# Fewer TensorE signals in a four-layer convolution kernel: second products, gate halves and encoding pairs

## The reference

```
layer 0: 2x2 patches as tokens; 8 experts, top 2 gated;
         out = out + gate[e] * ((val * sigmoid(g)) @ w2[e]),  val, g = split(xp @ w1[e])
layer 1: deformable 3x3 convolution (4 corners gathered per tap), batch norm, relu
layer 2: h = u @ W_enc + b_enc;  y = conv(h, K) + D * h;  g = gelu(y) @ W_glu + b_glu
         g = g[:256] * sigmoid(g[256:]);  out = layernorm(h + g) @ W_dec + b_dec
layer 3: depthwise 7x7 convolution, layer norm, MLP with gelu, scaled
```

## Time and profile before

| | us |
|---|---|
| median of 3 runs (1702.81 to 1703.12) | 1702.97 |
| span of the profiled execution | 2212.2 |
| difference | 509.2 |
| TensorE matmuls busy in it | 1480.2 |
| VectorE busy | 981.2 |
| ScalarE busy | 547.5 |
| GpSimd busy | 1208.5 |

### The profile page before, as it was taken

The page is one execution under the profiler, slowest core; times in us unless marked ns, Lnnn a source line. Parts: engine busy times, 40 slices in busy tenths (PEclk is TensorE's granted clock), DMA queues, the critical chain, the costliest instruction groups (busy, mean ns, idle before and its releaser), DMA issues.

```text
span 2212.2 us, 14137 instructions
## 1 busy us (share of the span) xinstructions
PE 1480.2 (67%) x4202; PEld 653.9 (30%) x4202; DVE 981.2 (44%) x1645; ACT 547.5 (25%) x874; POOL 1208.5 (55%) x1418
## 2 busy tenths in 40 slices
PE   7636651899645865957847765867847743665797
PEld 6432221343312322322313322322312311222245
DVE  3423342444422347842523247842431393323585
ACT  1111110233211231232322231231221302222446
POOL 8645455456465546566546546566546475565230
PEclk9867875899767887978967877978967985778899
DMA  6211221231212112321212112321212111211100
GB/s 198 56 52 49 55 55 51 69 91 51 60 46 75 47 37 60 82 58 43 68 33 77 51 37 59 82 59 43 59 40 56 29 50 40 64 42 49 31 8 13
DMA packets 111883, 123.08 MB, mean 56 GB/s; under 512 B 50880, under 2 KB 88896, under 8 KB 111424
## 3 DMA queue, kind: packets, MB, share of 16 engines
q0 software_dynamic: 36864, 75.57, 12.6%
q1 hardware_dynamic: 73888, 43.14, 7.6%
q10 hardware_dynamic: 1056, 3.47, 0.4%
HBM read 99.79 MB, written 9.01 MB: 49 GB/s over the span
## 4 chain that ended last, share of the span: by engine, by line
PE 33%; another core or an unknown queue 26%; DVE 17%; issue 15%; ACT 7%; DMA 1%; SPq 1%; DVEq 0%; ACTq 0%
PE bank L1960 6%; PE bank L1973 5%; DVE rb L1733 4%; PE bank L1875 4%; PE bank L1885 3%; PE bank L1867 3%; DVE gt L1617 3%; PE bank L1910 3%; PE bank L1943 2%; PE bank L1996 2%; DVE he L1515 1%; PE bank L1982 1%; DVE gt L1619 1%; DVE bst L1440 1%
## 5 line engine op out<-in xcount | busy, mean ns | idle before, releaser
L1137 POOL DMA_INDIRECT gt<-corner_table,idx x1152 | 1135.0, 985 | 877.1 <-DVE sm L1625 493.7
L1973 PE MATMUL bank<-yg,wts 128*128 128x512 f32 x512 | 252.2, 636 | 56.5 <-issue 30.9
L1960 PE MATMUL bank<-u,wk 128*128 128x512 f32 x512 | 254.0, 642 | 14.2 <-ACT yg L1298 4.0
L1659 DVE SCALAR_TENSOR_TENSOR tg<-tg,ae 128x512 f32<-128x512 f32 x64 | 44.4, 694 | 403.6 <-ACT ae L1310 342.0
L1875 PE MATMUL bank<-xg,w_sb 128*128 128x512 f32 (+1 forms) x288 | 156.1, 626 | 68.4 <-issue 38.9
L1515 DVE SCALAR_TENSOR_TENSOR he<-he,bank 128x512 f32<-128x512 f32 (+1 forms) x144 | 89.9, 626 | 206.0 <-remote 83.0
L1885 PE MATMUL bank<-he,w_sb 128*128 128x512 f32 (+1 forms) x288 | 150.1, 606 | 35.3 <-DVE he L1515 26.8
L1617 DVE TENSOR_TENSOR gt<-gt,bank 128x1152 f32<-128x1152 f32 x128 | 172.5, 1347 | 1.1
L1867 PE MATMUL bank<-xp,w_sb 128*128 128x512 f32 (+1 forms) x288 | 151.5, 610 | 20.3 <-ACT he L1212 13.6
L1212 ACT ACTIVATE he<-bank 128x512 f32<-128x512 f32 (+1 forms) x144 | 79.1, 549 | 307.6 <-PE bank L1867 157.3
L1733 DVE SCALAR_TENSOR_TENSOR rb<-xp,par,rb 128x1024 f32<-128x1024 f32 x124 | 155.1, 1292 | 0.0
(11 more groups left out here) (249 smaller groups left out, 1557.3 us busy)
## 6 DMA issues: line engine op xcount, KB each, us to landing
gt<-corner_table,idx POOLq DMA_INDIRECT x1152
tb<-gate_of_token SPq DMA_DIRECT2D x56, 256.0 KB
u<-sqb SPq DMA_DIRECT2D x48, 128.0 KB
corner_table<-tb SPq DMA_DIRECT2D x36, 128.0 KB, 2.9
w_sb<-w ACTq DMA_DIRECT2D x2, 1024.0 KB, 6.8
xp<-xg SPq DMA_DIRECT2D x56, 32.0 KB
X<-x SPq DMA_DIRECT2D x1, 1536.0 KB, 10.9
out<-X SPq DMA_DIRECT2D x6, 256.0 KB
```

The costliest lines, as they stand in the source:

```text
L1137: pool.indirect_dma_start(gt[:, t % GRING, k].rearrange("p a c -> p (a c)"), None, corners, bass.IndirectOffsetOnAxis(ap=idx[s % 2][:, j, ...
L1960: op = mm(psum[b][:, :], wk[:, t, d], u4[:, g, at:at + HALF], start=t == 0, stop=t == JJ - 1 and n > 0)
L1973: op = mm(psum[B2.bank(*name)][:, :], w_glu[:, k, col + d * P:col + (d + 1) * P], yg[:, c % 2, k], start=k == 0, stop=k == NB2 - 1)
```

## The change

Three signals are dropped, and the waits move to a later signal of the same bank semaphores. (1) A second product of layer 0 signals only when it closes its bank; `he_used`, the function `used` and ScalarE's wait for it are gone. (2) In `l2_g` gb has no signal of its own; whoever waits for gb waits for ga of the same d. (3) In `l2_z` only d = 1 signals; whoever waits for z(c, 0) waits for z(c, 1). A function `told_by` maps a result to the one that signals for it, and `Banks` counts signals and results apart. The order of instructions, the banks and all waits of TensorE stay.

```diff
-def used(a, u):
-
-    return sum(len(units(i)) // PAIR * (PAIR - 1) for i in range(a)) + u // PAIR * (PAIR - 1) + u % PAIR + 1
...
+def told_by(name):
+
+    kind, *k = name
+    if kind == "gb":
+        return ("ga", *k)
+    if kind == "z":
+        return ("z", *k[:-1], NB2 - 1)
+    return name
...
-        self.where, count = {}, {}
+        self.where, self.told, count, signals = {}, {}, {}, {}
         for name, bank in plan:
             self.where[name] = (bank, count.get(bank, 0))
             count[bank] = count.get(bank, 0) + 1
+            if told_by(name) == name:
+                signals[bank] = self.told[name] = signals.get(bank, 0) + 1
...
     def filled(self, eng, *name):
-        b, k = self.where[name]
-        eng.wait_ge(self.full[b], FROM + k + 1)
+        name = told_by(name)
+        eng.wait_ge(self.full[self.bank(*name)], FROM + self.told[name])
...
                 if u == PAIR + 1:
                     B0.filled(act, "out", a, 0)
-                elif u >= 2:
-                    act.wait_ge(S["he_used"], used(a, u - 2))
...
-                mm(psum[2][:, 0:w], w2_sb[:, e, h], he[:, u % 2, 0:w], start=first, stop=last)\
-                    .then_inc(full[2] if last else S["he_used"], 1)
+                op = mm(psum[2][:, 0:w], w2_sb[:, e, h], he[:, u % 2, 0:w], start=first, stop=last)
+                if last:
+                    op.then_inc(full[2], 1)
...
                         op = mm(psum[B2.bank(*name)][:, :], w_glu[:, k, col + d * P:col + (d + 1) * P],
                                 yg[:, c % 2, k], start=k == 0, stop=k == NB2 - 1)
-                    op.then_inc(full[B2.bank(*name)], 1)
+                op.then_inc(full[B2.bank(*name)], 1)
...
-                mm(psum[b][:, :], wenc[r, d * P:(d + 1) * P], u4[r, g, at:at + HALF], start=True, stop=True)\
-                    .then_inc(full[b], 1)
+                op = mm(psum[b][:, :], wenc[r, d * P:(d + 1) * P], u4[r, g, at:at + HALF], start=True, stop=True)
+                if d == NB2 - 1:
+                    op.then_inc(full[b], 1)
```

More of the change, by code:

```diff
@@ L777, in build @@
             var_ready0 var_ready1 var_ready2 var_ready3 std_ready0 std_ready1 std_ready2 std_ready3
-            xn0_ready xp_in o_in max_ready exp_ready gate_ready gate_out patch_ready he_used
+            xn0_ready xp_in o_in max_ready exp_ready gate_ready gate_out patch_ready
             xpad_ready rows_ready om_ready mask_ready idx_ready smp_ready relu_done
```

## The result

| | before | changed |
|---|---|---|
| median of 10 runs each, us | 1703.05 | 1709.01 |
| lowest and highest | 1700.48, 1707.14 | 1705.55, 1712.52 |
| ratio, 95% interval | | 1.0033 [1.0024, 1.0042] |
| span of the profiled execution | 2212.2 | 1707.2 |

The account below looks back on a forecast made before the run. Gathers and the work freeing their buffers were taken to share the bound. Signals 0, he_used 0, middle 5.4 and tail 2.2 made 7.6 us on 1702.97: 1710.6 us, range 1700 to 1716.

Parts of the forecast that it names:

- Signals: On TensorE, dropping 231 signals behind matmuls gains 0 us, 2.3 us at most.
- Rival (b): Signals hold TensorE, so dropping them makes the kernel faster, deciding from 0.048 us a signal: 1699.6 us; chance 0.13.
- he_used: ScalarE's dropped waits for second products in the first layer go for nothing: 0 us, at most 0.9 us to win.
- The bank: Second encoding behind the last ga waits for gb's later tanh: 0.89 us in five places, 0.40 in three, 5.7 us.
- The middle: Ahead of the tail, late closes and late-freed banks cost 0 to 10.7 us; half was taken, 5.4 us.
- The closes: Eight l2_close ahead of the tail each start up to 0.63 us late behind a later Identity: 5.0 us at most.
- 55.5 us in all: Median time's excess over a gather floor of 1647.5 us, made of 1152 gathers at 1.25 us plus both ends.
- rival (a): Gathers hide every delay in the middle and only the tail's 2.2 us remain: 1705.2 us; chance 0.32.
- TensorE's 80.96 of 85 us: TensorE's busy time from 460 to 545 us in the third layer, taken as a sign that TensorE binds there.
- The tail: At the end, no gather hides delays: Identity 0.63 us late, second rb 1.6 us late, together 2.2 us.

Follow-up runs that it names:

- only_he_used: Kernel before with only the 135 he_used signals and ScalarE's waits on them dropped: ratio 1.0007, 1704.94 us.
- bank_and_tail_kept: Changed kernel, but gb of d=1 keeps its signal while three banks rotate, and the last two channel parts keep all signals: ratio 1.0017, 1707.03 us.
- tail_kept: Changed kernel, but the last two channel parts keep their own signals for gb and both encodings: ratio 1.0017, 1707.48 us.
- only_encodings: Kernel before with only the first encoding told by the second one's signal: ratio 1.0009, 1705.57 us.
- only_gate_halves: Kernel before with only gb told by ga's signal: ratio 1.0020, 1708.40 us.
- before_again: The kernel before, unedited, timed and profiled once more: ratio 0.9997, 1703.49 us.

## Why the prediction was right, and where it was off

*Signals, 0 us: right.* 192 more leave the steps of their matmuls as they were, and 135 fewer (only_he_used) bring nothing that can be measured. Rival (b) is refuted.

*he_used, 0 us: nothing to gain, as said.* 1.0007 [0.9999, 1.0016]: no gain, and at most 2.7 us of loss, for which I know no mechanism.

*The bank: the mechanism and its size for TensorE right, its price wrong.* The pairs stretch in the eight places named, by 0.90 us in six of them; the three with a turn between lose 0.53, not 0.40, since what is lost there is the running side by side and not the wait. But the whole kernel pays nothing that can be measured: bank_and_tail_kept is level with tail_kept. The prediction called it "the largest term". With a third of the gathers left out the timed runs give it 7.3 us, which the traces don't confirm.

*The middle, 5.4 us: too large.* Measured is what tail_kept still has, 0.17%, 2.9 us, with an interval from 1.2 to 4.8. The closes' 5.0 us were 1.9 in the rows. The step that was off in what the gathers hide is the excess of "55.5 us in all": a floor made of 1.25 us a gather. The median gather is 0.944 us in the new profile too, but the mean is 0.997 (some take up to 2.43), and with the issue gap of 0.30 it is 1.30 us; 1152 x 0.05 = 58 us, the whole excess and a little more. The tail of 132.7 us held stops as well; it is 111. Made of the new rows, only the 20.9 us of waits are left to the matrix work. The median was the wrong duration for a sum over 1152 instructions, and the mean stood already on the page of the first profile, 985 ns:

```profile
L1137 POOL DMA_INDIRECT gt<-corner_table,idx x1152 | 1135.0, 985 | 877.1 <-DVE sm L1625 493.7
```

With it the excess of 55.5 us would have been 55.5 - 1152 x 0.038 = 12 us, which speaks for rival (a). TensorE's 80.96 of 85 us came from the execution with stops, in which GpSimd's gathers ran ahead or waited at other places than in a timed run, and said too little on what binds.

*The tail, 2.2 us: right.* 0.63 + 1.46 = 2.1 by the rows, plus 1.6 us of lower clock in the profiled executions that nothing in the forecast had.

*The sum.* Forecast 7.6 us, measured 5.6: 2.6 for the last two channel parts (tail_kept against the full change) and 2.9 elsewhere, to rounding. The sign, the order of the total and the tail came out as forecast. That the total is so near is partly luck: the 5.4 us were half of a bound that no row decided, its largest term isn't found in the time, and the 2.9 us that stand in its place have no known cause. For the bank, rival (a) had the mechanism right: a delay under the gathers is not paid. Its total, 1705.2, was too low, since something in the middle is paid all the same.

*What stays open.* The 2.9 us outside bank and tail. One candidate is the late Identity ahead of two closes (1.9 us), another he_used's 0.07%. A third is the gathers themselves. Their busy time varies from 1142.1 us (only_encodings) to 1151.2 (only_gate_halves), more than the difference sought, while the span less the tail and this busy time is 443 to 445 us in all ten profiled executions. Why 207 of the 1152 gathers take over 1 us (before_again), and whether the change makes them longer, no run tells. GpSimd's waits for buffers show 0.4 us of the difference.

## What to carry to other kernels

A signal that costs its engine nothing is worth keeping: here it frees a bank, or lets the next engine begin, 1.7 us earlier, and merging two into the later one only moves waits to places where something may stand behind them. Before summing a bound from a profile, look for stops in it, and sum over many instructions with the mean, not the median. A stall on a busy engine can cost nothing if that engine soon waits for a slower one. Cutting the slower one's work in a test kernel can show what it hides, but the clock and the tail move with such a cut, so it takes traces of several executions to tell what a difference is made of.

## What was unexpected in the hardware

A single execution can hold stops that no instruction of the kernel shows. On the chain of the first profile they are 93 pieces, half of them under 4.9 us and the longest 25.2; it spans 2212.2 us, all ten later profiles of whole kernels 1698.3 to 1710.1. They don't only add time, they move the waits: GpSimd's 493.7 us for buffers against 20.9.

The clock matters in a few microseconds of fillers: 44 products of 128 columns took 5.01 us at a granted clock of 1.00, and 6.64 us with 3.4 us of that stretch at the lower level, behind the same wait. That stretch fell into the tail in four of ten profiled executions, 1.6 us or 0.1% here.
